# A graph layer on one core: the low part of W1 times the high part of the edge sums as two row tiles of TensorE

## The reference

```
h   = maximum(layernorm(x), 0)
agg = segment_sum(edge_attr_48, dst, 12500)       # (12500, 48)
c   = concatenate([h, agg], axis=1)               # (12500, 176)
z   = silu(c @ W1 + b1)                           # W1 (176, 256)
z   = silu(z @ W2 + b2)                           # W2 (256, 256)
out = x + (h + z @ W3 + b3)                       # W3 (256, 128)
```

## Time and profile before

| what | value |
|---|---|
| median of three executions | 301.86 us |
| profiled execution | 301.52 us |
| its span, from first to last instruction | 299.8 us |
| PE busy | 282.7 us, 94% of the span |
| DVE busy | 249.6 us, 83% |
| ACT busy | 229.3 us, 76% |
| POOL busy | 113.8 us, 38% |

### The profile page before, as it was taken

The page is one execution under the profiler, slowest core; times in us unless marked ns, Lnnn a source line. Parts: engine busy times, 40 slices in busy tenths (PEclk is TensorE's granted clock), DMA queues, the critical chain, the costliest instruction groups (busy, mean ns, idle before and its releaser), DMA issues.

```text
span 299.8 us, 12214 instructions
## 1 busy us (share of the span) xinstructions
PE 282.7 (94%) x4378; PEld 258.8 (86%) x4379; DVE 249.6 (83%) x617; ACT 229.3 (76%) x435; POOL 113.8 (38%) x241
## 2 busy tenths in 40 slices
PE   6791998999999999999999999999999999999995
PEld 5681888899999999999999999999999999999794
DVE  7878897799888998889988898889988889875551
ACT  8773586787788877888778887888777887789662
POOL 3053554243433435334353334434444343532200
PEclk9888799999999999999999999999999999999999
DMA  6999076368655686557855678556875568731112
GB/s 164 303 286 254 4 218 181 94 191 245 209 155 159 215 245 191 157 151 235 245 170 150 178 237 237 158 156 184 244 230 159 147 200 245 205 104 33 33 32 58
DMA packets 79226, 52.94 MB, mean 177 GB/s; under 512 B 2949, under 2 KB 78815, under 8 KB 79205
## 3 DMA queue, kind: packets, MB, share of 16 engines
q1 hardware_dynamic: 79205, 52.70, 61.0%
HBM read 46.29 MB, written 6.40 MB: 176 GB/s over the span
## 4 chain that ended last, share of the span: by engine, by line
PE 81%; issue 5%; ACT 3%; DVE 3%; DMA 2%; POOL 2%; SPq 1%; POOLq 0%; ACTq 0%; DVEq 0%
PE agg_ps L1024 19%; PE z L1092 17%; PE z L1074 7%; PE z L1078 7%; PE z L1075 7%; PE z L1054 4%; PE stage L1027 4%; PE z L1056 4%; PE z L1059 4%; PE z L1060 4%; PE z L1055 4%; PE tp L1038 3%; DMA raw<-in_edge_attr_dram 2%; POOL agg_carry L443 2%; ACT xn L520 1%
## 5 line engine op out<-in xcount | busy, mean ns | idle before, releaser
L443 POOL TENSOR_TENSOR agg_carry<-staged,agg_carry 48x42 f32 x196 | 71.8, 366 | 90.8 <-ACT staged L489 61.2
L1024 PEld LDWEIGHTS agg_ps<-onehot,raw 128*48 128x48 f32 x1560 | 73.2, 126 | 9.4 <-issue 9.4
L1027 PE MATMUL stage<-onehot,raw 128*48 128x42 f32 x1568 | 77.2, 215 | 3.2 <-DMA raw<-in_edge_attr_dram 1.9
L705 DVE TENSOR_TENSOR onehot<-window,rel 128x1176 f32<-128x1176 f32 (+1 forms) x57 | 76.9, 1351 | 3.9 <-DVE stats L680 2.7
L1024 PE MATMUL agg_ps<-onehot,raw 128*48 128x42 f32 x1560 | 77.0, 215 | 0.0
L1027 PEld LDWEIGHTS stage<-onehot,raw 128*48 128x48 f32 x1568 | 73.6, 126 | 3.0 <-issue 3.0
L426 POOL TENSOR_TENSOR rstd<-vareps,minus_half 112x4 f32<-112x4 f32 (+1 forms) x28 | 38.8, 1384 | 75.9 <-DVE vareps L690 75.9
L1092 PE MATMUL z<-w,h 128*112 128x128 f32 (+1 forms) x448 | 55.9, 278 | 0.8 <-ACT h L552 0.8
L1092 PEld LDWEIGHTS z<-w,h 128*112 128x112 f32 (+1 forms) x448 | 50.4, 176 | 2.4 <-ACT z L548 1.1
L552 ACT ACTIVATE h<-z,b2c 128x448 f32<-128x448 f32 (+1 forms) x56 | 35.5, 634 | 20.0 <-PE z L1078 17.2
L520 ACT ACTIVATE xn<-x_t,nmr,rstd 112x128 f32<-112x128 f32 (+1 forms) x112 | 45.6, 478 | 0.5 <-DVE nmr L698 0.5
(11 more groups left out here) (122 smaller groups left out, 427.5 us busy)
## 6 DMA issues: line engine op xcount, KB each, us to landing
raw<-in_edge_attr_dram SPq DMA_DIRECT2D x55, 672.0 KB, 6.0
x_t<-in_x_dram SPq DMA_DIRECT2D x27, 224.0 KB, 6.1
out_dram<-out_t SPq DMA_DIRECT2D x27, 224.0 KB, 6.0
dst_rows<-in_dst_dram SPq DMA_DIRECT2D x1, 512.0 KB
raw<-in_edge_attr_dram SPq DMA_DIRECT2D x1, 288.0 KB, 3.5
dst_rows<-in_dst_dram SPq DMA_DIRECT2D x1, 256.0 KB, 2.7
out_t<-in_L_gnn_W_dram SPq DMA_DIRECT2D x1, 256.0 KB, 7.3
x_t<-in_x_dram SPq DMA_DIRECT2D x1, 192.0 KB
```

Source lines behind the costliest of these rows:

```text
L443: pool.tensor_tensor(into, staged[:, parity, n, :], into, ALU.add).then_inc(s_added, 1)
L705: return dve.tensor_tensor(onehot[:, slot, at * PER:n * PER, :], window[:, :].unsqueeze(1).broadcast_to([P, cols_n, WINDOW]), cols.unsquee ...
L1024: mm = pe.matmul(banks[0:ED, bass.ds(offsets[at - first], WINDOW)], edges, into, start=False, stop=True, skip_group_check=True, tile_posit ...
L1027: mm = pe.matmul(stage[ROW2:ROW2 + ED, at * WINDOW:(at + 1) * WINDOW], edges, into, start=(at == 0 and j == 0), stop=True, skip_group_chec ...
```

## The change

The last matmul of each half (L1060) is taken out of the two groups of five. After both halves' four matmuls come two instead, one per half, each on 48 partitions: half 0 with `w1e_lo` and `agg_hilo` in partitions 0 to 47 at tile position (0, 0), half 1 with a second copy of `w1e_lo` and of the sums' high part in partitions 64 to 111 at tile position (64, 0). They are two row tiles of the array and write different banks of PSUM. The last node tile keeps the form of before.

For that, DVE computes the second copy of `w1e_lo` once at the start, and ACT writes the second copy of the sums' high part for each tile (`agg_hi_again`) after relu. On ACT, `seed_b3` and half of the normalization move ahead of `activate1`. On DVE, `aggregate_stats` moves ahead of the first `h1_lo_part`.

```diff
+        agg_hi_below = sb("agg_hi_below", [ROW2 + ED, TILE], F32R)
...
+            def agg_hi_again(t):
+                n = PER * nodes_p(t)
+                act.wait_ge(s_agg, t + 1)
+                wait(act, s_z1, M * t)
+                act.activation(agg_hi_below[ROW2:ROW2 + ED, 0:n], agg[:, 0:n], ACT.Copy).then_inc(s_agg_below, 1)
...
+                first = isinstance(i, int) and i == 1
                 last = isinstance(i, int) and i >= NT - 1
+                if has(i, 1, NT - 1):
+                    agg_hi_again(i - 1)
...
                 if has(i, 2, NT):
                     activate2(i - 2, 1)
+                if has(i, 2, NT) and not last:
+                    seed_b3(i - 2)
+                if has(i, 0, NT) and not last and not first:
+                    normalize(i, turn, range(0, PER // 2))
                 if has(i, 1, NT):
                     activate1(i - 1)
-                if has(i, 2, NT) and not last:
-                    seed_b3(i - 2)
-                if has(i, 0, NT) and not (isinstance(i, int) and i == NT - 1):
+                if first:
                     normalize(i, turn)
+                elif has(i, 0, NT) and not last:
+                    normalize(i, turn, range(PER // 2, PER))
...
-                        (w1e_lo[0:ED, :], w1e_in[0:ED, :], w1e_hi[0:ED, :])):
+                        (w1e_lo[0:ED, :], w1e_in[0:ED, :], w1e_hi[0:ED, :]),
+                        (w1e_lo[ROW2:ROW2 + ED, :], w1e_in[ROW2:ROW2 + ED, :], w1e_hi[ROW2:ROW2 + ED, :])):
...
+                if has(i, -1, NT):
+                    aggregate_stats(i + 1, 1 - parity)
                 if has(i, 1, NT):
                     h1_lo_part(i - 1, 0)
-                if has(i, -1, NT):
-                    aggregate_stats(i + 1, 1 - parity)
...
+                last = isinstance(t, int) and t == NT - 1
...
-                    pe.wait_ge(s_w_lo, 3)
+                    pe.wait_ge(s_w_lo, 4)
...
-                    pe.matmul(z[:, m, 0:n], w1e_lo[:, cols], agg_hilo[:, 0:n],
-                              start=False, stop=True).then_inc(s_z1, 1)
+                    if last:
+                        pe.matmul(z[:, m, 0:n], w1e_lo[:, cols], agg_hilo[:, 0:n],
+                                  start=False, stop=True).then_inc(s_z1, 1)
+                if last:
+                    return
+                pe.wait_ge(s_agg_below, t + 1)
+                pe.matmul(z[:, 0, 0:n], w1e_lo[0:ED, 0:P], agg_hilo[0:ED, 0:n],
+                          start=False, stop=True, tile_position=(0, 0)).then_inc(s_z1, 1)
+                pe.matmul(z[:, 1, 0:n], w1e_lo[ROW2:ROW2 + ED, P:2 * P], agg_hi_below[ROW2:ROW2 + ED, 0:n],
+                          start=False, stop=True, tile_position=(ROW2, 0)).then_inc(s_z1, 1)
```

More of the change, by code:

```diff
@@ L233, in gnn_kernel @@
         s_agg_lo = sem("agg_lo_ready")
+        s_agg_below = sem("agg_hi_below_ready")
         s_w_hi = sem("weights_hi_ready")
@@ L509, in _, with normalize @@
                 act.activation(w1e_hi[a:a + ED, :], w1e_in[a:a + ED, :], ACT.Copy).then_inc(s_w_hi, 1)
-            def normalize(i, turn):
+            def normalize(i, turn, quarters=range(PER)):
                 np_ = nodes_p(i)
@@ L518, in normalize @@
                 wait(act, s_plain, i - 1)
-                for q in range(PER):
+                for q in quarters:
                     ln = act.activation(xn[0:np_, parity, q, :], x_t[0:np_, turn, q, :], ACT.Identity,
                                         bias=nmr[0:np_, parity, q:q + 1], scale=rstd[0:np_, parity, q:q + 1])
-                ln.then_inc(s_xn, 1)
+                if quarters[-1] == PER - 1:
+                    ln.then_inc(s_xn, 1)
             def relu(t):
```

## The result

The changed kernel takes 307.46 us (median of 4 runs, 305.59 to 307.83) against 301.71 us of the kernel before: a ratio of 1.0187 with a 95% interval of 1.0133 to 1.0241. Run once more beside other kernels it took 306.78 us against 301.88, a ratio of 1.0164 (1.0121 to 1.0207). So it is slower: by 5.75 us in the first comparison (its interval is 4.0 to 7.3 us) and by 4.90 us in the second. The forecast was 307.1 us.

The account below looks back on a forecast made before the run. PE's queue was taken to set each step. 4.3 (middle) + 0.34 + 0.3 (start) + 0.6 (end) = 5.5 us on 301.52 gave 307.0, forecast 307.1 from the median; own range 305.3 to 308.6, 8 in 10 range 301.9 to 310.0.

Parts of the forecast that it names:

- PE sets the step: Middle steps: a step of 9.48 us is as long as PE's queue; ACT's work is free until PE waits.
- The removal gives 0.03 of 0.20: Layer 1, half 1: its load waits for ACT to empty the bank, so only 0.03 of 0.20 us arrives.
- The pair costs 0.71 against 0.49: From half 1's L1077 to the sums: changing to row tiles and an exposed load make 0.71 us against 0.49.
- The mark read off the 7-row matmul: Load of L1132 starts 0.07 us before the L1130 matmuls end, taken as the sign that changed tile rows empty the array.
- B: Rival at the way into row tiles: a change of rows empties nothing; 302.2 us, or 302.5 from the median; chance 0.15.
- D: Rival around the pair: neither change of division costs anything; 0.15 us less in each of 24 steps, 298.5 us; chance 0.10.
- A step is 0.18 longer: Middle steps: 0.22 us added by the pair less 0.03 gained, less 0.01 for rounding; 24 steps make 4.3 us.
- Both row tiles side by side: The pair in layer 1: the second tile's load runs beside the first's and adds 0.01 us.
- Rival C: The pair: the second tile follows the first; 309.7 us if its load waits, 311.8 if its matmul does; chance 0.18.
- The start, 0.34 + 0.3: Kernel start: 0.34 us for DVE's extra `weights_lo` piece, 0.3 for one more change of division in step 1 at lower clock.
- ACT and DVE cost nothing in the middle: Middle steps: `agg_hi_again` is hidden, and `activate1` starting 1.2 us later is covered by waits and 0.88 us of room.
- The end, 0.6: Step 27: `activate1` starts 1.7 us later, waits take most of it; 0.6 us taken between bounds 0.2 and 1.2.

Follow-up runs that it names:

- e2: Changed kernel with PE's matmuls in the order of before and `activate1` waiting for both halves; middle step 9.471 us, median 304.45 us.
- e3: Changed kernel with half 1 of layer 1 in a PSUM bank of its own; middle step 9.463 us, median 302.20 us.
- e8: Kernel before with half 0's L1060 as a row tile on partitions 0 to 47 between whole matmuls; middle step 9.850 us, 312.17 us in one run.
- e5: Changed kernel with half 1's last matmul on the same row tile as half 0's; middle step 9.840 us, 313.95 us in one run.
- e7: Kernel before with only the second copy of `w1e_lo` added, computed by DVE and waited for by PE; median 302.26 us, ratio 1.0009.
- e10: Changed kernel run once more without edit; median 306.78 us, ratio 1.0164 to the kernel before.
- e6: Changed kernel with the form of before for the last two node tiles; last two distances 8.72 + 6.12 us, 304.85 us in one run.
- e1: Changed kernel with two whole matmuls in place of the pair of row tiles; middle step 9.643 us, median 306.15 us.
- e9: Kernel before with an extra PSUM bank for half 1 and 22 unread matmuls in PE's wait for the first `hT_lo`; median 298.52 us, ratio 0.9894.

## Why the prediction was right

Point by point, by its own steps:

- *PE sets the step.* Right: PE is busy for 9.62 of 9.62 us, and e2 moved all of ACT's and DVE's work without moving the step.
- *The removal gives 0.03 of 0.20.* Right: 0.04 is given (1.03 to 0.99), and e3 takes the wait away and gets 0.16. That the bank is free for tile 1 was wrong: its half 1 waits for ACT too, 0.26 us at 41.86, so the loss begins one tile earlier than counted.
- *The pair costs 0.71 against 0.49.* Right in mechanism, 0.02 too much: 0.69 (0.29 and 0.40). The mark read off the 7-row matmul held for row tiles of 64, and e8 shows it with nothing else changed. Rivals B and D, by which that change empties nothing, are out: e8 would have stood at 9.5 or below.
- *A step is 0.18 longer.* Mis-sized: 0.15. The 0.03 are the 0.02 of the pair and 0.01 of the gain; 24 steps make 3.6 to 3.7 instead of 4.3 us.
- *Both row tiles side by side.* Right (0.01 apart; e5 costs 0.21 more). Rival C is out.
- *The start, 0.34 + 0.3.* Mis-sized in its first term: DVE's extra piece took 0.45 and the piece before it 0.11 more, and layer 1 of tile 0 begins 0.57 later behind DVE's first weight piece (8.02 against 7.45 us) in the changed kernel and in e7. Its cost in the total stays open (e7, e10), and so does the second term: no run shows the 0.3 for one more change of division at a lower clock.
- *ACT and DVE cost nothing in the middle.* Right, by the margin worked out (e2: 9.471): DVE's `agg` now follows its second h_lo without a wait, where it had waited 0.70 for the sums, and starts 0.14 later in the step. ACT's split of it now idles for 0.54 us instead of 0.27, which PE doesn't feel:

```profile
152.99 0.62 DVE L890 TENSOR_TENSOR h_lo<-h,h_hi 128x448 fp32r<-128x448 f32 x1 [0.51 <-ACT h_hi L573]
153.54 0.62 DVE L866 TENSOR_TENSOR agg<-agg_ps,agg_carry 48x448 f32<-48x448 f32 x1
```

- *The end, 0.6.* The mechanism is right (e6). The size, 0.64 against 0.6, was picked between the bounds 0.2 and 1.2 and not worked out, so that it fits so well is luck.

Three terms, put together as an estimate, account for the middle steps of all these kernels to about 0.01 us: 0.167 for the wait for half 1's bank (e1 less the kernel before), 0.187 for one more change of division (half of e8's addition), and 0.212 saved by the overlap (e5 less the mean of the changed kernel's two). From 9.476 they give 9.618 for the changed kernel (measured 9.624 and 9.632), 9.830 for e5 (9.840) and 9.451 for e3 (9.463).

The total of 307.1 met 307.46 and 306.78, but not as closely as that looks. The prediction's terms add up to 5.5 us; the second comparison measured 4.9 and the first 5.75, with intervals of 1.3 and 1.6 us to either side. The middle was counted 0.6 to 0.7 us too high, and nothing shows that another term made up for it. The lower end of the range doesn't follow from its terms either: 24 x 0.14 + 0.6 leads to 305.5 us, not 305.3.

## What to carry to other kernels

Two matmuls side by side are worth something only above the price of the way in and out: here 0.19 us for each change of the array's division, against 0.20 us saved. One such change came on top, because the sums behind were column tiles already; between whole matmuls it would be two. Before an instruction is taken out of the queue that sets the time, look at the one behind it and at what that one waits for; a wait that one matmul had hidden took back 0.16 of the 0.20 us. And read the weight loads, not only the matmuls: both waits of this case stand there.

## What the runs showed of the hardware

- A matmul of 448 columns declared as a row tile of 64 between whole matmuls costs 0.374 us more (e8), 0.187 per change of division, about the same on the way in and on the way out.
- A weight load that had to wait is paid on top of the wait: the matmul behind it takes 0.47 instead of 0.36 us (149.08 in the changed kernel, 281.19 before).
- A start-up wait of PE costs more than itself: with 22 matmuls in it whose result nobody reads, the granted clock stayed at the level of 2.4 GHz and 2.4 us were saved (e9). The spread of the totals may come in part from the same place, which isn't shown. For it: e9's four runs differ by 0.33 us, those of the other experiments by 0.65 (e10) to 2.9 (e2); e2's five runs with a mean granted clock of 0.977 or 0.978 took 304.83 to 305.37 us and its five at 0.989 302.44 to 304.07; and e5, whose low clock lasted longest (25.8 to 39.4 us of its span, against 26.4 to 33.2 in the changed kernel), reached layer 2 of tile 0 3.0 us later than the changed kernel. Against it: runs at the same 0.989 still differ by 1.6 us in e2.
- The Trainium skill's rule that a change of tiling mode drains the engine (TensorEngine Tiling (Array Packing), Tiling Modes) agrees with e8 and its 0.187 us. The same skill's model of a pack as one matmul's time and some 4 ns for each further tile (TensorE: Matmul & The Clock Gate, Part 3) agrees with the trace in the distance of the two tiles, 3 to 4 ns in all 27 pairs. What the pair takes in its place is more than that model counts: from L1077 to the loads of the sums 0.69 us, where one whole matmul took 0.49.
